# Both attention stages: class value products in bf16 of three parts, first heads loaded during the stage before

## What is computed

```python
# layer 0: causal ReLU attention
scores = einsum(q, k) / sqrt(16); att = relu(scores) * causal
att = att / (att.sum(-1) + 1e-9);  ctx = einsum(att, v)
# layer 1: softmax attention over all positions, class token included
ctx = softmax(q k^T / sqrt(16)) v
```

## Time and profile before

| | |
|---|---|
| median of 3 runs | 2316.9 us (2316.5 to 2319.5) |
| profiled execution | 2317.5 us, span of its instructions 2315.7 us |
| busy, share of the span | PE 2132.0 (92%), DVE 1591.6 (69%), ACT 898.2 (39%), POOL 677.5 (29%) |
| fp32 class products, causal stage | 32 products, 36.8 us of PE |
| fp32 class products, last stage | 32 products, 36.8 us of PE |
| projection stage, causal stage, last stage | about 168 to 315, 315 to 556, 1801 to 2316 us |

### The profile page before, as it was taken

How to read it: one execution, slowest core, us unless ns; L and a number is a source line. 1 busy time by engine, 2 the same in 40 slices (tenths; PEclk the granted TensorE clock), 3 DMA queues, 4 the chain that set the end, 5 groups by cost and what they waited for, 6 DMA issues and landing times. The chain is left out here.

```text
span 2315.7 us, 40942 instructions
## 1 busy us (share of the span) xinstructions
PE 2132.0 (92%) x11635; PEld 1349.1 (58%) x11635; DVE 1591.6 (69%) x4349; ACT 898.2 (39%) x2108; POOL 677.5 (29%) x1282
## 2 busy tenths in 40 slices
PE   7998969998999997999978949999999899999998
PEld 6877833334888885666653327888888223333332
DVE  3336846664777766888858856777776778888881
ACT  1114635553122224444424422222222067777777
POOL 3554525553333422333321101111111311111111
PEclk9998979998999999999989969999999589999999
DMA  3324664552000000000010001112212512222210
GB/s 126 117 86 94 150 183 131 139 138 89 1 0 0 0 0 14 0 0 0 0 54 9 9 27 38 43 40 46 46 38 45 141 34 75 75 75 75 75 43 20
DMA packets 215001, 131.95 MB, mean 57 GB/s; under 512 B 117186, under 2 KB 203916, under 8 KB 214924
## 3 DMA queue, kind: packets, MB, share of 16 engines
q1 hardware_dynamic: 214924, 131.01, 21.1%
HBM read 89.51 MB, written 40.93 MB: 56 GB/s over the span
## 5 line engine op out<-in xcount | busy, mean ns | idle before, releaser
L2474 DVE TENSOR_REDUCE attend_mx<-ps 128x1 f32<-128x512 f32 x512 | 326.0, 683 | 71.7 <-PE ps L2195 70.3
L2332 ACT ACTIVATE keep_x<-ps 128x512 f32<-128x512 f32 x512 | 280.7, 596 | 125.4 <-PE ps L2209 123.9
L1839 PE MATMUL ps<-keep_early,moe_zT 128*128 128x256 f32 x1056 | 243.3, 384 | 6.4 <-DVE keep_h L1994 4.4
L1839 PEld LDWEIGHTS ps<-keep_early,moe_zT 128*128 128x128 f32 x1056 | 196.5, 191 | 43.1 <-DVE keep_h L1994 18.6
L2195 PE MATMUL ps<-attend_ks,keep_o 96*128 96x512 bf16 x512 | 209.4, 414 | 9.0 <-DVE attend_mx L2474 4.7
L2209 PE MATMUL ps<-keep_o,attend_ks 99*128 99x512 bf16 x512 | 191.9, 384 | 2.2 <-ACT keep_x L2332 2.2
L857 DVE SCALAR_TENSOR_TENSOR keep_early<-ps,causal_causal 128x512 f32<-128x512 f32 (+3 forms) x256 | 114.1, 486 | 82.9 <-PE ps L737 82.8
L1994 DVE SCALAR_TENSOR_TENSOR keep_h<-ps,moe_g,keep_h 128x256 f32 (+1 forms) x264 | 127.5, 483 | 61.1 <-PE ps L1839 52.7
L2195 PEld LDWEIGHTS ps<-attend_ks,keep_o 96*128 96x128 bf16 x512 | 50.4, 99 | 195.9 <-DVE attend_mx L2474 148.9
L827 POOL TENSOR_TENSOR keep_early<-keep_early,causal_causal 128x128 f32<-128x128 f32 x256 | 113.0, 457 | 131.8 <-ACT keep_early L796 130.8
L796 ACT ACTIVATE keep_early<-ps 128x512 f32<-128x512 f32 (+3 forms) x256 | 98.5, 435 | 129.1 <-PE ps L737 128.9
(11 more groups left out here) (325 smaller groups left out, 4024.8 us busy)
## 6 DMA issues: line engine op xcount, KB each, us to landing
tok_xin<-in_xk SPq DMA_DIRECT2D x64, 256.0 KB, 2.8
qk_parts<-qkv_parts SPq DMA_DIRECT2D x33, 384.0 KB, 3.2
qk_parts<-moe_parts SPq DMA_DIRECT2D x33, 384.0 KB, 3.2
causal_qs<-qk_parts SPq DMA_DIRECT2D x96, 128.0 KB, 2.6
causal_ks<-qk_parts SPq DMA_DIRECT2D x96, 128.0 KB, 2.7
keep_o<-qk_parts SPq DMA_DIRECT2D x96, 128.0 KB, 2.8
attend_ks<-qk_parts SPq DMA_DIRECT2D x96, 128.0 KB, 2.8
v_all<-qkv_v SPq DMA_DIRECT2D x33, 136.0 KB, 3.1
```

Source lines behind the costliest of these rows:

```text
L1839: last = nc.tensor.matmul(ps[:, E0 + pair % 2, e % 2 * D:(e % 2 + 1) * D], zT[:, u, k * P:(k + 1) * P], we[e][:, k, :], start=(k == 0), st ...
L2332: nc.scalar.activation(w[:, j, kt % 2, :], ps[:, SC + (HG * k + j) % RING, :], ACT.Exp)\
L2474: nc.vector.tensor_reduce(mx[:, t, k:k + 1], ps[:, MX + (TB * k + t) % RING, :], AX, ALU.max)\
```

## The change

1. Causal and last stage: the class product is one bf16 matmul. Weights and class values are each split into three bf16 parts, and six pairs of parts (`PQ`, `PK`) are stacked in rows: 8 heads x 6 = 48 rows in the causal stage; 72 in the last one (48 in use; the groups begin at rows 0, 32 and 64).
2. The block-diagonal class values (`vb`) are no longer made by a matmul and DVE, but by DMAs that write the parts of the row into a zeroed DRAM array with a row pitch one head longer than its content, and read it back. The zero fill stands in `pass_constants`.
3. `pass_qkv` splits the class weights (three POOL operations per tile) and tile 0's class values (four), and `class_out` is issued one tile later.
4. The first half of batch 0 of the causal stage, its constants, and four units of the last stage are loaded by the preceding pass within its last six tiles. In the last stage `ks` moves to `env.x`, v and `room` to `early[1]`, `w` gets an area of its own.
5. In the causal stage the load of a half has `LOADS` = 19 DMAs instead of 14.

```diff
 # pass_constants, SP
+            sp.dma_start(flat, blank.bitcast(BF16)[:, 0:flat.shape[1]]).then_inc(env.s_blank, 16)
...
+            sp.dma_start(flat, blank[:, 0:flat.shape[1]]).then_inc(env.s_blank, 16)
 # pass_qkv, SP
-            for s, u, n in tiles(sp, 5):
+            for s, u, n in tiles(sp, 5, LATE):
...
-                if known(s) >= 1:
-                    class_out(s, u)
+                if known(s) >= 2:
+                    class_out(s - 1, 1 - u)
+                if isinstance(s, int) and s == 4:
+                    class_value_rows()
+                if isinstance(s, int) and s == NT - LATE:
+                    for w in range(2):
+                        sp.wait_ge(s_out[w], 16 * 3)
+                        sp.wait_ge(s_vout[w], 16 * 3)
+                        sp.wait_ge(s_cout[w], 16 * 2)
+                    ahead.first.load_stacks(sp, io, 0)
+                if isinstance(s, int) and s == NT - LATE + 1:
+                    sp.wait_ge(s_diag, 16 * 6)
+                    ahead.first.load_values(sp, io, 0)
+                    ahead.load_constants(sp, io)
+            class_out(NT - 1, (NT - 1) % 2)
 # pass_qkv, ACT
-                nc.scalar.activation(cls_s[:, u, :], ps[0:NH, 6 + u, 0:P], ACT.Relu).then_inc(s_cls, 1)
+                nc.scalar.activation(cls_s[:, u, :], ps[0:NH, 6 + u, 0:P], ACT.Relu)
+                nc.scalar.activation(cls_p[:, u, 0, :], ps[0:NH, 6 + u, 0:P], ACT.Relu).then_inc(s_cls, 1)
 # pass_qkv, POOL, per tile
+            def class_parts(s, u):
+                ch = Chain(pool, c_cls, 2 * (s - 1))
+                pool.wait_ge(s_cls, s)
+                pool.sem_inc(s_took, 1)
+                ch.link(nc.gpsimd.tensor_tensor(cls_r[:, :], cls_s[:, u, :], cls_p[:, u, 0, :], ALU.subtract))
+                pool.sem_inc(s_took, 1)
+                ch.link(nc.gpsimd.tensor_copy(cls_p[:, u, 1, :], cls_r[:, :]))
+                pool.sem_inc(s_took, 1)
+                nc.gpsimd.tensor_tensor(cls_p[:, u, 2, :], cls_r[:, :], cls_p[:, u, 1, :], ALU.subtract).then_inc(s_clsp, 1)
+                pool.wait_ge(s_clsp, s)
+                pool.sem_inc(s_took, 1)
...
                     third(s - 3, 1 - u)
+                if known(s) == 3:
+                    class_value()
+                if known(s) >= 4:
+                    class_parts(s - 3, 1 - u)
 # the load of a half, causal stage (class Half; load_stacks is the loop of 12 as before)
+    def load_values(self, sp, io, b):
+        heads = slice(self.n * HALF, (self.n + 1) * HALF)
+        sp.dma_start(self.v[:, :, :], io["v_all"][bass.ds(1 + TB * b, TB), :, heads.start * (HD + 1):heads.stop * (HD + 1)]
+                     .rearrange("n p f -> p n f")).then_inc(self.sem, 16)
+        for c, part in enumerate(PQ):
+            sp.dma_start(self.cls[HALF * c:HALF * (c + 1), :],
+                         io["cls_parts"][part, heads, bass.ds(TB * b, TB), :].rearrange("h n t -> h (n t)"))\
+                .then_inc(self.sem, 16)
 # pass_causal, SP (before: v0, own, pick, causal and both halves)
+            halves[1].load_stacks(sp, io, 0)
+            halves[1].load_values(sp, io, 0)
+            sp.dma_start(v0[:, :], io["v_all"][0, 0:B, :]).then_inc(s_w, 16)
             env.ahead["mlp"].start(sp)
 # pass_causal, PE
+                nc.tensor.matmul(ps[:, 4 + g % 2, :], vb[:, g // 2, at:at + 2 * HD * HG], halves[g // 2].cls[:, :],
+                                 start=True, stop=False, skip_group_check=True)
 # pass_moe, SP
+                unit = s - (NT - LATE) if isinstance(s, int) else -1
+                if unit == 0:
...
+                    env.heads.load_class(sp, io)
+                if 0 <= unit < 4:
+                    env.heads.load(sp, io, unit // 2, unit % 2, unit)
 # pass_attend, PE
-                    nc.tensor.matmul(ps[:, CTX, :], vbdc[:, half, 2 * HD * HG * g:2 * HD * HG * (g + 1)],
-                                     cw[:, half, :], start=True, stop=False, skip_group_check=True)
+                    nc.tensor.matmul(ps[:, CTX, :], vb[:, b, half, 2 * HD * HG * g:2 * HD * HG * (g + 1)],
+                                     cwp[:, half, :], start=True, stop=False, skip_group_check=True)
 # pass_attend, ACT
-                    nc.scalar.activation(cw[:, u, :], turned[QR:QR + HALF, :], ACT.Exp).then_inc(s_cw, 1)
+                    past(act, s_cwp, c)
+                    nc.scalar.activation(cw[:, :], turned[0:CR, :], ACT.Exp)
+                    nc.scalar.activation(cwp[:, u, :], turned[0:CR, :], ACT.Exp).then_inc(s_cw, 1)
 # pass_attend, POOL, per unit, behind parts(x): four operations of 512 columns on up to 72 rows
+            def class_weights(x):
...
+                ch.link(nc.gpsimd.tensor_tensor(cw[:, :], cw[:, :], cwp[:, u, :], ALU.subtract))
...
+                ch.link(nc.gpsimd.tensor_copy(cwp[32:64, u, :], cw[32:64, :]))
...
+                ch.link(nc.gpsimd.tensor_copy(cw1[64:CR, :], cw[64:CR, :]))
...
+                nc.gpsimd.tensor_tensor(cwp[64:CR, u, :], cw[64:CR, :], cw1[64:CR, :], ALU.subtract).then_inc(s_cwp, 1)
 # pass_attend, DVE, largest: three subtractions into GROUPS = ((0, 3), (32, 2), (64, 1)) instead of one
+                for r, n in GROUPS:
+                    nc.vector.tensor_tensor(
+                        side[:, :, r:r + HALF * n].rearrange("p t (a h) -> p t a h", a=n),
...
```

More of the change, by code:

```diff
@@ L444, in pass_qkv @@
         cls_s = a.sb("cls_s", [NH, 2, P])
+        cls_r = a.sb("cls_r", [NH, P])
+        cls_p = a.sb("cls_p", [NH, 2, 3, P], BF16)
+        v0p = a.sb("v0p", [1, 3, NH * (HD + 1)], BF16)
+        v0r = a.sb("v0r", [1, NH * (HD + 1)])
+        s_clsp, c_cls, s_v0p, c_v0, s_diag = (a.sem(n) for n in ("clsp", "c_cls", "v0p", "c_v0", "diag"))
+        ahead = env.causal
+        LATE = 6
         v = a.sb("v", [P, 2, NH, HD + 1])
@@ L674, in pass_causal @@
+CONSTS = 16 * (1 + len(PK))
 def pass_causal(nc, env, io):
@@ L2157, in _ @@
                     sp.sem_inc(s_took, 1)
-                    load(x.b(-2), x.half(2), x.buf(2))
+                    heads.load(sp, io, x.b(-2), x.half(2), x.buf(2))
                 if x.has(1):
```

318 lines of the change are left out of this document (204 added, 114 removed).

## The result

The changed kernel takes 2350.4 us (median of 4 runs, 2349.3 to 2351.1); the kernel before, beside it, 2318.2. The ratio is 1.0139, 95% interval 1.0121 to 1.0156. The forecast was 2337, slower with chance 0.70, range 2300 to 2362. Direction and range were right, the terms only in part.

A forecast was written before the change was run, and what follows sets the result against it. PE seemed to bound the projection, causal and last stages, with causal load and work nearly balanced. From 2317.53 us, -32.6 + 25.4 + 11.9 + 2 + 12.4 + 0.5 = +19.6 gave 2337.1, stated as 2337, range 2300 to 2362.

The forecast's parts named there:

- Projection stage, POOL: Projection stage: added operations make POOL the bound, 4.10 us a tile, 11.9 us over 22 tiles plus 2 near tiles 3 and 4.
- the upper end: Projection stage: if DVE and POOL exclude each other for whole instructions, the top of 3.85 to 4.4 us a tile, 7 us more.
- End of SP's queue: Projection stage's last six tiles: early loads delay stores and casts, 12.4 us lost, of which class splits are 4.
- Causal stage, load chain: Causal stage: five added class DMAs lengthen each serial load by 2.5 us; with clock, 13 x 3.0 = 39 us lost.
- The clock's share: Causal stage: a lower clock after PE's idle gaps costs up to 1.3 us an interval, taken as 0.5.
- The gain at the start: Causal stage: with the first half already loaded, the load for batch 1 lands sooner, 11.7 us gained.
- Last stage: Last stage: cheaper class product 22.0 us and early loads net 10.6 us, together 32.6 us gained (26 to 38).
- The product's stretch: Last stage: score to score across one bf16 class product takes 0.44 us instead of 1.36, 0.92 saved twice per unit.
- two slots paced by DVE: Last stage: two slots each get 0.45 us of longer subtractions, making the early loads' 11.5 us a net 10.6.
- With small gaps ... hidden: Expert stage's last tiles: SP's stores and early loads take 10.3 us within tiles of some 12 us, so no cost.
- Rival 4: Causal stage: PE's idle gaps leave the clock at 0.50 for most of each half, 13 intervals at 18.2 us, 2361; chance 0.12.
- Rival 3: POOL bounds the projection stage, but causal loads are not later because issue overlaps landing: 2274 us; chance 0.10.

The follow-up runs named there:

- experiment 1: Changed kernel, but in the projection stage ACT takes the class scores of tile s-3 ahead of the zT copy of tile s: 2329.7 us.
- experiment 2: Changed kernel without POOL's three class split operations per tile in the projection stage; the store waits for ACT instead: 2301.6 us (one run).
- experiment 3: Changed kernel with POOL's class split one tile later in the projection stage (tile s-4), ACT's order kept: 2311.4 us.
- experiment 9: Changed kernel with the edits of experiment 3 and experiment 8 together: 2283.4 us.
- experiment 10: Experiment 9 with the projection stage's 26 early loads spread three per tile from tile 23 on, not packed behind tiles 27 and 28: 2273.9 us.
- experiment 8: Changed kernel; in the causal stage SP loads a half's stacks after its last scores, only v_all and class weights wait for its last values: 2321.4 us.
- experiment 6: Changed kernel with the causal stage's class weights loaded for the first batch only, 13 DMAs per later half instead of 19: 2333.7 us (one run).
- experiment 7: Changed kernel with the six class-weight DMAs issued ahead of their half's stacks in the causal loop, not behind v_all: 2374.5 us (one run).
- experiment 12: Changed kernel with the last stage's first four halves loaded at that stage's start again, not in the expert stage: 2359.1 us (one run).
- experiment 11: Experiment 10 with v_all and class weights issued between the first and last six stack DMAs of a half in the causal loop: 2287.4 us.
- experiment 5: Changed kernel with three DMAs instead of six per half for the causal stage's class weights, same bytes and rows: 2351.6 us.

## Why the forecast was right in sign and wrong in its terms

**Projection stage, POOL** ("POOL becomes the bound ... I take 4.10, 0.54 per tile for 22 tiles: 11.9 us"). This is the step that failed. It costed the new operations by their durations alone, and these were right to 0.04 us each. It did not follow the wait that came with them. A split on POOL waits for an activation on ACT, and behind it stands the next tile's statistics: the term should have been a latency, from 248.18 round to 253.58, not a sum of busy time. Measured 1.92 us a tile for 25 tiles, 47.9 us, where 11.9 was forecast, and 3.7 instead of 2 at the start. Experiments 1 to 3 show it: moving the split by one tile gives back 39 us and lands at 4.18, close to the 4.10 forecast.

The Trainium skill (SBUF — State Buffer, "SBUF: two separate sides") has DVE in a two-port mode and GpSimd shut each other out for a whole instruction, and by it the stage would have stood at the upper end. In experiment 3 L632 takes 0.628 us for 0.417 where it meets DVE's L688 and the cast L690 (264.57), and z takes 1.13 us at the median for 0.41 while L621 runs on POOL. So the trace agrees that the two engines hold each other up. But the cost to POOL is 0.21 us a tile in the mean, where the cast takes 0.43, and the steady pace was 4.09: the stage did not come to that end.

**End of SP's queue** (12.4): measured 12.9, but only 4.9 are the loads. At the fast pace packing the same loads behind two tiles costs 9.9 us more than spreading them (experiments 9 and 10), near the 8.4 that the forecast had without the class splits. So the reasoning holds where the ring doesn't cover the loads.

**Causal stage, load chain** ("per added DMA I take 0.50 ..., five of them 2.5 us"). The mechanism was right, experiment 8 shows it by opening the chain; the size was wrong. Six DMAs take SP 2.31 us, 0.385 each. More important, I added the whole issue to a chain that ends in a landing, and left the landing as it was. Before, the scores followed the last issue by 2.7 us (458.72 to 471.06, last issue ended at 468.40): that is the landing of the one fp32 class load of 32 KB, and v_all, issued 0.6 us ahead of it, lands at about the same time (2.9 us from issue to landing for each of the two). The last of the six small loads is in use 1.25 us after its issue, so 1.4 us of the 2.0 us of longer issue are made up for. How much v_all's landing hides, experiment 6 shows: without any class loads the load is still 12.1 us (experiment 7 has the opposite order). The clock's share was 0.3 us an interval, 0.5 forecast: SP's next load is released 1.6 to 2.6 us after the scores of a first half, instead of 1.6. So 13 intervals cost 15.3 us instead of 39. The gain at the start was 13.3 (11.7 forecast), at the end 0.7 (1.8).

**Last stage** (-32.6, measured -36.8). The product's stretch is 0.44 us as forecast, score to score across it, where the earlier trace rows had 1.36:

```profile
2068.33 0.38 PE L2347 MATMUL ps<-keep_o,keep_x 99*128 99x512 bf16 x1
2068.55 0.38 PE L2358 MATMUL ps<-attend_cwp,attend_vb 72*128 72x512 bf16 x1
2068.77 0.38 PE L2333 MATMUL ps<-keep_x,keep_o 96*128 96x512 bf16 x1
```

A unit gained 1.42 us (1.44). The maxima start 0.9 us behind the stage's first instruction, 11.8 sooner (11.5). What is left, some 6.5 us in the first slot and the last units, I had put at 2.4 (3.3 less the 0.9 for two slots paced by DVE); where the rest comes from was not looked into. "With small gaps ... hidden" for the loads in the expert stage held (experiment 12): the stage's +3.2 us are a lower clock near its start, a term that the forecast did not have.

**Rivals.** Rival 4 (slower by the clock) has its mechanism behind most first halves, but at 0.3 us an interval in the mean, not the 1.35 that it needs. Its 2361 also counts from 16.35 us and leaves out the 0.5 already charged; 13 times 18.2 less 16.85 gives 2355. Rival 3 (the class loads don't come later) was nearer to the causal stage than the forecast, but its POOL term was the same as mine. None of the five had a ring.

## What to carry to other kernels

Where an operation is added to an in-order queue, write down whom it waits for and who stands behind it on its own engine, and follow both until they meet: if they do, the pace is the length of the ring divided by the tiles that it spans (here 5.4 us over one tile, and 9.3 over two in experiment 1). A stage in which no engine is full (here PE at 70%) and one wait returns in every tile is a sign of such a ring; here, shifting the new work by one tile opened it. In these load chains the small transfers belong last: what is issued while the large one lands costs little, and the same DMAs with the large one last cost 24 us. And before a small difference in a stage is put down to an edit, look at the same stage in the other kernels.

## What the runs showed of the hardware

- For the class weights SP's issue was not cheaper in fewer DMAs: six of 8 rows of 1 KB took 2.31 us, three for the same 48 rows 2.20 to 2.22. Rows alone don't set it: a stack load of 128 rows took 0.58 us, v_all (272 KB) 0.46.
- Behind the seven waits of 2.5 to 3.7 us in the changed kernel the first group of heads took 7.6 to 9.1 us instead of 6.0 (first four score matmuls 1.03 to 1.89 us for 1.03). Of the waits of 1.2 to 2.2 us in experiment 6 none was followed by that; of six of 1.7 us in experiment 11 three were, each at about 9.1. So a wait of 2.6 us costs 4.2 to 5.7 in all, part of which the next load uses.
- The same idle gap of 4.4 us at the expert stage's start was followed by 10 us at a granted clock of 0.51 in the changed kernel and of 0.84 in experiment 5: 3.1 us of difference with the same work.
- The small class loads, issued behind v_all, were in use 1.25 us after the end of their issue; v_all, when last, 2.5 to 2.9 us; the one 32 KB class load of before 2.5 to 2.8; a 128 KB stack load, when last (experiment 11), 2.2.
- DVE's z (128x256) took 1.01 to 1.24 us while POOL's 128x512 subtraction ran and 0.41 us with POOL free; that subtraction stayed at 1.15.
